# Perceiver block on one core: query rows stacked inside SBUF, a finer weave in the last context chunk, biases loaded early, branch sides exchanged

## The reference

```python
x = x + cross(layernorm(x), ctx)      # ctx: 25088 x 512
x = x + self_attn(layernorm(x))
x = x + ffn(layernorm(x))

# cross: q = x @ Wq.T * 32**-0.5, k = ctx @ Wk.T, v = ctx @ Wv.T
#        out = (sigmoid(q k^T) v) @ Wo.T           (no softmax, so no row sums)
# self:  qk = x @ Wqk + bqk, v = x @ Wv + bv, n = x @ Wn + bn
#        out = ((q k^T * tril) / exp(n)) v @ Wo + bo
# ffn:   h = silu(x w1^T s1) * (x w2^T s2); h = gelu(h h1^T sh1)
#        h = gelu(h h2^T sh2); out = h w3^T s3     (w: -1, 0 or 1)
```

## Time and profile before

| | |
|---|---|
| median of 3 runs | 2024.51 us (2022.19 to 2024.71) |
| the profiled execution | 2024.97 us |
| its span, first to last instruction | 2023.2 us |
| granted TensorE clock, mean | 0.992 |
| TensorE matmuls busy | 1986.7 us, 98% |
| TensorE weight loads busy | 1779.1 us, 88% |
| VectorE busy | 1213.5 us, 60% |
| ScalarE busy | 1008.6 us, 50% |

### The profile page before, as it was taken

The page is one execution under the profiler, slowest core; times in us unless marked ns, Lnnn a source line. Parts: engine busy times, 40 slices in busy tenths (PEclk is TensorE's granted clock), DMA queues, the critical chain, the costliest instruction groups (busy, mean ns, idle before and its releaser), DMA issues. The chain is left out here.

```text
span 2023.2 us, 50736 instructions
## 1 busy us (share of the span) xinstructions
PE 1986.7 (98%) x19372; PEld 1779.1 (88%) x19372; DVE 1213.5 (60%) x2113; ACT 1008.6 (50%) x1132; POOL 4.3 (0%) x16
## 2 busy tenths in 40 slices
PE   7999999999999999999999999999999999988999
PEld 6888999888899988889998888999888899856998
DVE  5566566666656666665666666566666656235322
ACT  3445455454545545454554545455454545533764
POOL 0000000000000000000000000000000000000000
PEclk9999999999999999999999999999999999998999
DMA  5655655555565555556555555656555554543774
GB/s 181 142 153 151 160 137 155 142 142 151 150 159 137 156 141 142 151 150 159 137 156 141 143 151 150 159 137 156 140 143 151 149 149 108 137 154 127 270 286 160
DMA packets 127939, 311.96 MB, mean 154 GB/s; under 512 B 33720, under 2 KB 33720, under 8 KB 108856
## 3 DMA queue, kind: packets, MB, share of 16 engines
q1 hardware_dynamic: 95784, 215.93, 41.2%
q10 hardware_dynamic: 32112, 95.43, 15.1%
HBM read 155.52 MB, written 1.57 MB: 78 GB/s over the span
## 5 line engine op out<-in xcount | busy, mean ns | idle before, releaser
L337 ACT ACTIVATE probs<-sc 128x1024 f32<-128x1024 f32 x784 | 760.4, 1023 | 777.0 <-PE sc L712 770.4
L676 PE MATMUL kp<-x_combos,weights_r 128*128 128x256 f32 x4032 | 539.9, 284 | 0.9 <-DVE k_rows_lo L519 0.9
L676 PEld LDWEIGHTS kp<-x_combos,weights_r 128*128 128x128 f32 x4032 | 509.3, 193 | 1.2 <-issue 1.2
L712 PE MATMUL sc<-rows_r,k_stack_r 96*128 96x256 f32 x3136 | 453.8, 288 | 13.3 <-issue 10.7
L697 PE MATMUL vp<-more_weights,x_combos 128*128 128x256 f32 x3456 | 461.4, 283 | 0.0
L712 PEld LDWEIGHTS sc<-rows_r,k_stack_r 96*128 96x128 f32 x3136 | 405.3, 193 | 56.0 <-issue 52.0
L697 PEld LDWEIGHTS vp<-more_weights,x_combos 128*128 128x128 f32 x3456 | 435.5, 192 | 0.0
L729 PE MATMUL acc<-probs,v 128*32 128x256 f32 x6272 | 361.0, 382 | 0.1
L532 DVE TENSOR_TENSOR parts<-parts,kp 128x512 f32<-128x512 f32 x240 | 164.6, 686 | 310.8 <-PE kp L676 310.8
L729 PEld LDWEIGHTS acc<-probs,v 128*32 128x32 f32 x6272 | 194.4, 110 | 131.7 <-issue 1.1
L467 DVE TENSOR_TENSOR x_combos<-ctx_raw,x_combos 128x512 fp32r<-128x512 f32 x235 | 162.7, 692 | 8.0
(11 more groups left out here) (163 smaller groups left out, 997.0 us busy)
## 6 DMA issues: line engine op xcount, KB each, us to landing
k_stack_r<-k_rows_hi SPq DMA_DIRECT2D x784, 64.0 KB, 2.3
k_stack_r<-k_rows_lo SPq DMA_DIRECT2D x784, 64.0 KB, 2.0
k_stack_r<-k_stack_r SPq DMA_DIRECT2D x196, 256.0 KB, 3.0
ctx_raw<-ctxT_dram ACTq DMA_DIRECT2D x47, 1024.0 KB, 5.8
piece<-w_all_dram ACTq DMA_DIRECT2D x176, 256.0 KB, 5.2
w_raw<-w_all_dram SPq DMA_DIRECT2D x44, 1024.0 KB, 4.8
weights<-wqk_dram SPq DMA_DIRECT2D x2, 1024.0 KB, 11.0
rows_r<-q_rows SPq DMA_DIRECT2D x3, 512.0 KB, 7.8
```

Source lines behind the costliest of these rows:

```text
L337: nc.scalar.activation(probs[:, t % 2, g, :], sc[g % 2][:], ACT.Sigmoid).then_inc(probs_ready, 1)
L676: last = nc.tensor.matmul(k2[:, r, :], wk[i - 1][:, k, a, r * P:(r + 1) * P], xc[:, i - 1, k, b, :], start=i in FRESH and n == 0, stop=n = ...
L712: last = nc.tensor.matmul(sc[g % 2][:, j * L:(j + 1) * L], kst[0:3 * D, t // 2, g // 2, j, g % 2, t % 2 * P:(t % 2 + 1) * P], qst[0:3 * D, ...
```

## The change

Four edits, independent of each other.

1. The query rows go straight from `qr_hi` and `qr_lo` into the stacked tile: four transfers of 32 partitions for the high rows, four for the low rows, and one copy of the high band to the second band, in the manner of `stack_rows`. The HBM tensor is gone. TensorE's wait counts 5 x 16 in place of 3 x 16.
2. In the last chunk, TensorE scores pair p + 1 and then weighs the two (t, g) of pair p, for p = 0 to 7.
3. The four small loads of self-attention, and their tiles, move into cross-attention's SP queue, behind the reload of x and ahead of the chunks.
4. The condition of both branches is turned round, so that the exact side stands first. VectorE's final multiply and add move into both sides.

```diff
+            def stack_queries():
+                to = f32(qst[:, :, :, :])
+                sp.wait_ge(q_hi, 1)
+                for j in range(HG):
+                    sp.dma_start(to[0:D, j, :, :], as_groups(qr_hi)[D * j:D * (j + 1)]).then_inc(q_moved, 16)
+                sp.wait_ge(q_lo, 1)
+                for j in range(HG):
+                    sp.dma_start(to[2 * D:3 * D, j, :, :], as_groups(qr_lo)[D * j:D * (j + 1)]).then_inc(q_stacked, 16)
+                sp.wait_ge(q_moved, MOVED)
+                sp.dma_start(to[D:2 * D], to[0:D]).then_inc(q_stacked, 16)
+
             stack_rows(0, 0)
             sp.wait_ge(q_made, 1)
             sp.dma_start(raw1, ctxT[1]).then_inc(ctx1_loaded, 16)
-            sp.wait_ge(q_hi, 1)
-            sp.dma_start(kept_q[0].rearrange("d j g l -> j d g l"), f32(qr_hi)).then_inc(q_kept, 16)
-            sp.wait_ge(q_lo, 1)
-            sp.dma_start(kept_q[1].rearrange("d j g l -> j d g l"), f32(qr_lo)).then_inc(q_kept, 16)
-            sp.wait_ge(q_kept, 32)
-            sp.dma_start(f32(qst[0:D, :, :, :]), kept_q[0]).then_inc(q_stacked, 16)
-            sp.dma_start(f32(qst[D:2 * D, :, :, :]), kept_q[0]).then_inc(q_stacked, 16)
-            sp.dma_start(f32(qst[2 * D:3 * D, :, :, :]), kept_q[1]).then_inc(q_stacked, 16)
+            stack_queries()
             for q in range(1, 4):
                 stack_rows(0, q)
             sp.dma_start(x1[:], x_rows).then_inc(x_loaded, 16)
+            wn, bqk, bn, bo = biases
+            sp.dma_start(keep["wn"][:], wn).then_inc(keep["bias_loaded"], 16)
+            sp.dma_start(keep["bqk"][:], bqk).then_inc(keep["bias_loaded"], 16)
+            sp.dma_start(keep["bn"][:], bn).then_inc(keep["bias_loaded"], 16)
+            sp.dma_start(keep["bo"][:], bo.partition_broadcast(P)).then_inc(keep["bias_loaded"], 16)
...
-                for n, g in ((n, g) for n, (tile, g) in enumerate(order) if tile == t):
+                for n, g in ((n, g) for n, (tile, g) in enumerate(order) if tile == t and g in groups):
...
-                last.then_inc(probs_used, 1)
+                if G - 1 in groups:
+                    last.then_inc(probs_used, 1)
...
-            pe.wait_ge(q_stacked, 3 * 16)
+            pe.wait_ge(q_stacked, MOVED + 16)
...
                 if not k_next:
-                    for p in range(3):
-                        pair(p)
-                    for t in range(TC):
-                        weigh(c, par, t, BY_TILE)
-                        for p in (2 * t + 3, 2 * t + 4):
-                            if p < 2 * TC:
-                                pair(p)
+                    pair(0)
+                    for p in range(2 * TC):
+                        if p + 1 < 2 * TC:
+                            pair(p + 1)
+                        weigh(c, par, p // 2, BY_TILE, groups=range(p % 2 * 2, p % 2 * 2 + 2))
                     return
...
-            sp.dma_start(wn_sb[:], wn).then_inc(bias_loaded, 16)
-            sp.dma_start(bqk_sb[:], bqk).then_inc(bias_loaded, 16)
-            sp.dma_start(bn_sb[:], bn).then_inc(bias_loaded, 16)
-            sp.dma_start(bo_sb[:], bo.partition_broadcast(P)).then_inc(bias_loaded, 16)
...
                 units(dve, one)
+                for a in range(LT):
+                    dve.wait_ge(y_made, a + 1)
+                    nc.vector.tensor_tensor(y[:, a, :], py[a][:], s3_sb[:], ALU.mult).then_inc(y_step, 1)
+                    dve.wait_ge(y_step, a + 1)
+                    nc.vector.tensor_tensor(y[:, a, :], y[:, a, :], x2[:, a, :], ALU.add).then_inc(y_ready, 1)
 
             dve.wait_ge(keep["inexact_ready"], 1)
             count = nc.vector.value_load(keep["any_inexact"][:], min_val=0, max_val=P)
-            with dve.If(count > 0):
+            with dve.If(count < 1):
+                hidden(exact=True)
+            with dve.Else():
                 hidden(exact=False)
-            with dve.Else():
-                hidden(exact=True)
...
-            with pe.If(count > 0):
+            with pe.If(count < 1):
+                multiply(exact=True)
+            with pe.Else():
                 multiply(exact=False)
-            with pe.Else():
-                multiply(exact=True)
```

More of the change, by code:

```diff
@@ L103, in keep_clock, with cross_attention @@
         nc.tensor.matmul(to, zeros[:, 0:P], zeros[:], start=True, stop=True, skip_group_check=True)
-def cross_attention(nc, x, ctxT, wqT, wkT, wvT, woT, wqk, wv, bv, wo, w_all, kept_q, keep):
+def cross_attention(nc, x, ctxT, wqT, wkT, wvT, woT, wqk, wv, bv, wo, w_all, biases, keep):
     ident, x1, qst, next_weights = keep["ident"], keep["x1"], keep["rows"][0], keep["weights"][1]
@@ L152, in cross_attention, with as_groups @@
         qr_hi, qr_lo = (parts_r[:, 2 * b:2 * b + 2, :, :].rearrange("p a r n -> p (a r n)") for b in range(2))
+        def as_groups(rows):
+            return f32(rows).rearrange("p (g l) -> p g l", g=G)
         w21 = v_r[:, 1, :, :].rearrange("p a n -> p (a n)").rearrange("p (w k b n) -> p w k b n", w=2, k=2, b=2)
@@ L169, in cross_attention @@
         bv_loaded, v1_made, v1_ready = sem("bv_loaded"), sem("v1_made"), sem("v1_ready")
-        q_hi, q_lo, q_kept, q_stacked = sem("q_hi"), sem("q_lo"), sem("q_kept"), sem("q_stacked")
+        q_hi, q_lo, q_moved, q_stacked = sem("q_hi"), sem("q_lo"), sem("q_moved"), sem("q_stacked")
         wk_summed, wv_summed = sem("wk_summed"), sem("wv_summed")
@@ L715, in scores, with weigh @@
                 last.then_inc(scores_ready, 1)
-            def weigh(c, par, t, order, first=False):
+            def weigh(c, par, t, order, first=False, groups=range(G)):
                 if t % 2 == 0 and first:
@@ L870, in _, with self_attention @@
             v_self(1, vp)
-def self_attention(nc, bqk, wn, bn, bo, scales, s3, w_all, keep):
+def self_attention(nc, scales, s3, w_all, keep):
     ident, x1, x2, x_hi, x_lo = keep["ident"], keep["x1"], keep["x2"], keep["x_hi"], keep["x_lo"]
@@ L889, in self_attention @@
         wq_sb, wk_sb, wo_sb = (keep["weights"][1][:, i, :, :] for i in range(1, 4))
-        wn_sb, bqk_sb = sb("wn_sb", [P, KE, H]), sb("bqk_sb", [P, 2 * KE])
-        bo_sb, bn_sb, bn_neg = sb("bo_sb", [P, E]), sb("bn_sb", [H, 1]), sb("bn_neg", [H, 1])
+        wn_sb, bqk_sb, bo_sb, bn_sb = keep["wn"], keep["bqk"], keep["bo"], keep["bn"]
+        bn_neg = sb("bn_neg", [H, 1])
         xnT = keep["xnT"]
@@ L914, in norm_of @@
             return xT_psum[:, a, :].rearrange("p (k l) -> p k l", k=KE)
-        bias_loaded = sem("bias_ld")
+        bias_loaded = keep["bias_loaded"]
         mask_one, heads_one, heads_step, const_ready = (
@@ L1404, in build @@
         keep["v"] = rows[:, 2, :, :].rearrange("p g l -> p (g l)").rearrange("p (a n) -> p a n", a=LT)
-        kept_q = nc.dram_tensor("q_rows", (2, D, HG, G, L), F32, kind="Internal").ap()
-        cross_attention(nc, x, ctxT, wqT, wkT, wvT, woT, wqk, wv, bv, wo, w_all, kept_q, keep)
+        keep |= {"wn": sb("wn_sb", [P, KE, H]), "bqk": sb("bqk_sb", [P, 2 * KE]), "bo": sb("bo_sb", [P, E]),
+                 "bn": sb("bn_sb", [H, 1]), "bias_loaded": sem("bias_ld")}
+        cross_attention(nc, x, ctxT, wqT, wkT, wvT, woT, wqk, wv, bv, wo, w_all, (wn, bqk, bn, bo), keep)
         keep |= {"any_inexact": sb("any_inexact", [1, 1], mybir.dt.int32), "inexact_ready": sem("any_inexact_ready"),
@@ L1413, in build @@
                  "w_rounded": sem("w_rounded"), "w_split": sem("w_split")}
-        self_attention(nc, bqk, wn, bn, bo, (s1, s2, sh1, sh2), s3, w_all, keep)
+        self_attention(nc, (s1, s2, sh1, sh2), s3, w_all, keep)
         mlp(nc, w_all, out, keep)
```

## The result

| | before | after |
|---|---|---|
| median | 2024.32 us (6 runs, 2022.19 to 2024.71) | 1956.12 us (6 runs, 1955.23 to 1957.34) |
| profiled execution, span | 2024.97, 2023.2 us | 1955.81, 1954.1 us |
| mean granted clock | 0.992 | 1.0 |

The ratio is 0.9665, 95% interval 0.9653 to 0.9677. The forecast was 2000.8, range 1996.5 to 2006.5. The change brought 68 us where I had counted 24.

The account below looks back on a forecast made before the run. The prediction took TensorE to bound the kernel for nearly the whole span. Its terms, 14.5 + 3.2 + 3.0 + 3.3 + 0.7 - 0.5 = 24.2 us, taken from 2024.97 gave 2000.8 us, range 1996.5 to 2006.5.

Parts of the forecast that it names:

- Part 1: Before the first scores: stacking query rows without HBM removes TensorE's stall; gain 14.5 us, bounds 10.7 and 14.6.
- The landing of the query rows: At the start: the 32-partition transfers of query rows were taken to land in 2.1 us, leaving nearly 6 us of cover.
- Part 2: Last chunk in couples: TensorE becomes the bound, ScalarE is covered; gain 3.2 us, bounds 1.3 and 4.6.
- its two cases: Last chunk: gain 4.5 us if the clock stays full, 1.8 if it falls to half speed.
- Part 3: Start of self-attention: early small loads remove TensorE's wait for a bias; gain 3.0 us, bounds 2.4 and 3.0.
- Part 4: Before the MLP: exact side first shortens the 6.37 us idle by 3.3, clock 0.7 more, end jump costs 0.5.
- 2.0 + 1.6 = 3.6, less some 0.3: Before the MLP's first matmul: instruction fetch request to landing 2.0, then resuming 1.6, less the matmul's own wait; gain 3.3 us.
- 0.7 for the clock: MLP's start: of 3.0 us lost to half-speed clock, 0.7 comes back, since some 3 us of idle remain.
- The bounds 6.4 and 3.0: Upper bounds at the MLP's start: 6.4 us gained from the idle before its first matmul, 3.0 from the clock.
- The jump at the other end: End of the span: VectorE must skip the inexact side after its last add; cost 0.5 us, bounds 0 and 2.
- more comes back than I count: Rival: no clock fall in the last chunk, MLP starts at full clock; gain 27.8 us, 1997.2 us; chance 0.17.
- theory Q: From the follow-ups, not the prediction: operand distance modulo 128 sets matmul pace; 64 apart is fast, 0 apart slow.

Follow-up runs that it names:

- pad2368: The kernel before with one unused tile of 2368 bytes a partition where the change puts its bias tiles: 1985.8 us, ratio 0.981.
- after_front: The changed kernel with its four bias tiles allotted ahead of all others, restoring the old distances between big tiles: 1993.65 us, ratio 0.9849.
- pad2304: The kernel before with one unused tile of 2304 bytes a partition where the change puts its bias tiles: 2023.4 us, ratio 1.0.
- pad128: The kernel before with one unused tile of 128 bytes a partition where the change puts its bias tiles: 2015.1 us, ratio 0.9958.
- skew_all: The changed kernel with four unused pads of 32 or 64 bytes, meant to set all loop and MLP operand pairs 64 apart modulo 128: 1949.8 us, ratio 0.9638.

## Why the prediction was wrong

**The step that failed** stands in its first part: "The loop over the chunks, some 1,690 us of the span, is not touched, and there TensorE waits for nothing worth a term." Both halves are true of the instructions, and the conclusion is not. Edit 3 touched the loop through its operands' distance. The cost of an operation was taken from rows of before as if it belonged to the operation; it belonged to the operation and the distance of its two operands. Worth 37.6 of the 44 us that were missing; shown by pad2368, by after_front and by pad2304. In all my terms I had treated a tile's move as costing nothing, and never asked what lies between which tiles.

**Part 1** was right in mechanism and size: 14.4 for 14.5, and 14.4 in the run of edit 1 alone (2024.1 - 2009.7), in whose trace the second pair starts at 46.60 for the forecast 46.67. In the changed kernel two small things cancel: the new distances bring the first scores 0.4 forward, and of the 0.93 wait for key rows 0.46 is left. The landing of the query rows was mis-sized, 4.9 for 2.1, within cover.

**Part 2** was right in mechanism and had the wrong one of its two cases: the stretch gained 4.7 (4.6 with the edit alone), where I had 4.5 if the clock holds, with a bound of 4.6, and forecast the middle, 3.2. That the medians with the edit alone show 3.4 is no proof of the middle, as said above. Why the clock holds there now isn't shown. The five steps take 2.09 to 2.32 with one of 2.63 that contains the wait of 0.28; their mean is 2.26 where I had 2.28. That is partly luck: the two groups with the switch take 1.00 for my 1.14, and some pairs of scores 1.28 (1711.09 to 1712.37) for 1.14.

**Part 3** was right as far as it went: 3.0 for the wait.

**Part 4**: the step mis-sized was "2.0 + 1.6 = 3.6, less some 0.3". The whole idle of 6.37 hung on the order of the sides: 0.16 is left. I had kept 3 us for reading the flag and deciding. They don't show: with the exact side next in order the first matmul comes 0.16 behind four keep-alive matmuls that last 1.02. So the 3 us in front of the packets of the earlier trace rows belonged to the branch as well. What fills them isn't shown; the loads of weights took 98.4% of the DMA engines' time in the window of those packets. The changed kernel has no instruction packet from 1772 to 1784, around the same place. The second term, 0.7 for the clock, followed from the same error. With no idle, the clock stayed at full speed, and the first layer took 30.30 for 33.27. Of these 3.0, 2.7 is the clock (30.55 with edit 4 alone), more than in most other runs of the old order, and 0.25 the new distances. The bounds 6.4 and 3.0 had been named, and the traces came close to both. That a page of the Trainium skill ("Runtime: NRT & Kernel Launch", Instruction fetch mechanics) says a taken branch out of the held pages waits for a fetch fits these packets; the Trainium skill's 108 ns for a compare-and-branch ("Advanced Engine Details and Errata", Control Flow Timing) is not what was paid here. The jump at the other end is real in the trace, but cheap: an instruction packet lies in 1950 to 1952, where the kernel before has none in its last 3 us, and the span ends 3.33 behind the last add in place of 3.12, so 0.2 for my 0.5, beside the landing of the output.

The packet, from the DMA queues in that window:

```profile
q14 instruction: 1, 0.01, 1.1%
```

Of the rivals, "more comes back than I count" was the nearest in kind, with 27.8 us against the 31.5 that the change brings without the loop. Even a forecast with every one of the four parts right would have missed by 37.6.

**What stays open.** Why the loss comes back every 128 bytes, and not quite: pad128 gains 8.4 us that theory Q doesn't give. Why most value products stop at about 1.41 at a distance at which key products reach 1.37, and what else than its own two tiles sets an operation's pace. Why skew_all's runs lie between 1945 and 1950, further apart than those of the other kernels. I haven't tried distances between 64 and 128 or any larger than 2496, nor pairs one at a time. That the cause is the stationary operand's load reading the same part of the memory as the moving operand is argued from which pairs react. No run measured such reads by themselves.

## What to carry to other kernels

Before a kernel that TensorE bounds is costed, list the addresses of the stationary and the moving operand of its hot matmuls, and treat any edit that allots, drops or resizes a tile as an edit of every tile behind it. Tiles whose sizes are all multiples of 128 bytes stood at the worst distance measured here; an unused tile of 64 bytes in the right place is a test that costs a line, and here it was worth more than the four edits' own effects together. The branch out of line at the start of a stage was worth turning round here: 6.2 us of idle, and 1.3 to 2.7 more of slow clock behind it.

## What the runs showed of the hardware

The pace of fp32r matmuls with 128 columns of weights and 256 moving columns depended on the distance of their operands in a partition: a group of twelve key products took 1.44 us with 0 or 2304 bytes added between the operands, 1.43 with 128 or 2432, 1.41 with 32 and 1.37 with 64, 2368 or 2496. A chunk took 35.40 (0 and 2304 bytes added), 35.17 (128), 34.97 (32) and 34.63 (64 and 2368). The Trainium skill ("TensorE: Matmul & The Clock Gate", Step-by-step: what each phase is for) says that loading the next weights doesn't steal read bandwidth from the running matmul, since there are two independent ports. By that the distance should make no difference, and here it made one of 5% of the key products' time; the measurement decides. That it is the loads that take something from the matmuls is argued, not shown. Weighings with 32 columns of weights showed nothing of it (381 ns at either distance).
